# Attention in a fused three-layer kernel: the max pass two quarters ahead of the exp pass, shift rows placed quarter by quarter

## Time and profile before

| | us |
|---|---|
| median of three runs | 835.84 |
| the three runs | 838.26, 829.43, 835.84 |
| the profiled execution | 830.55 |
| its span, first to last instruction | 828.8 |

### The profile page before, as it was taken

One profiled execution on the slowest core, in us unless ns is written; L12 is line 12 of the kernel. 1 busy time (PEld: TensorE's weight loads), 2 busy tenths in 40 slices (PEclk: granted clock), 3 DMA queues, 4 the chain that ended last, 5 costly groups with the idle time before them and its releaser, 6 DMA issues.

```text
span 828.8 us, 23658 instructions
## 1 busy us (share of the span) xinstructions
PE 780.3 (94%) x6498; PEld 380.8 (46%) x6498; DVE 746.7 (90%) x2543; ACT 629.5 (76%) x1529; POOL 539.0 (65%) x838
## 2 busy tenths in 40 slices
PE   3999999989999999999999999999999998999997
PEld 2545544434444444454454454444444444445443
DVE  4899989989999999999999999999999848999996
ACT  2777777626888888888888888888878766677775
POOL 3787877865567566567567567467453336878887
PEclk9999999977999999999999999999999999999999
DMA  6700000332333233233233233233231000010011
GB/s 172 133 0 0 0 1 20 112 133 93 107 118 105 90 118 106 86 115 108 83 115 111 81 115 115 77 115 117 80 120 36 2 1 15 26 38 25 25 38 39
DMA packets 54969, 62.02 MB, mean 75 GB/s; under 512 B 5696, under 2 KB 48576, under 8 KB 54784
## 3 DMA queue, kind: packets, MB, share of 16 engines
q1 hardware_dynamic: 54912, 61.33, 23.2%
HBM read 31.70 MB, written 29.36 MB: 74 GB/s over the span
## 4 chain that ended last, share of the span: by engine, by line
PE 53%; DVE 16%; issue 7%; POOL 3%; ACT 2%; DVEq 1%; POOLq 0%; ACTq 0%
PE bank L1004 17%; PE bank L964 11%; DVE att_neg_max L1198 8%; PE bank L987 6%; PE bank L1019 4%; PE bank L1043 2%; PE bank L1023 2%; DVE x L561 2%; PE bank L303 2%; PE bank L310 2%; PE bank L967 2%; POOL moe_rstd L419 1%; DVE x L1241 1%; PE bank L1034 1%; PE bank L1017 1%
## 5 line engine op out<-in xcount | busy, mean ns | idle before, releaser
L1198 DVE TENSOR_REDUCE att_neg_max<-bank 128x1 bf16<-128x512 f32 (+3 forms) x704 | 407.9, 637 | 23.7 <-PE bank L967 20.2
L1077 ACT ACTIVATE att_probs<-bank 128x512 f32<-128x512 f32 x640 | 346.8, 596 | 64.1 <-PE bank L987 62.9
L1158 POOL TENSOR_SCALAR_AFFINE_SELECT att_probs<-att_probs 128x512 f32<-128x512 f32 x256 | 159.3, 634 | 201.1 <-ACT att_probs L1077 200.8
L987 PE MATMUL bank<-att_q_st,att_k_st 53*128 53x512 bf16 (+3 forms) x1024 | 210.6, 302 | 1.1 <-ACT att_probs L1077 1.1
L374 ACT ACTIVATE moe_scaled<-bank,moe_gates 128x128 f32<-128x128 f32 x512 | 145.2, 370 | 62.8 <-PE bank L310 57.0
L964 PE MATMUL bank<-att_k_st,att_q_st 51*128 51x384 bf16 (+2 forms) x768 | 180.3, 280 | 6.1 <-DVE att_neg_max L1198 4.6
L1004 PE MATMUL bank<-att_probs,att_v 128*32 128x512 f32 (+3 forms) x2048 | 177.3, 441 | 1.0 <-POOL att_probs L1158 0.4
L561 DVE SCALAR_TENSOR_TENSOR x<-bank,moe_gates,x 128x128 f32 (+1 forms) x512 | 160.4, 339 | 16.6 <-PE bank L303 15.7
L967 PE MATMUL bank<-att_k_st,att_q_st 64*128 64x128 bf16 x1024 | 159.3, 220 | 0.1
L964 PEld LDWEIGHTS bank<-att_k_st,att_q_st 51*128 51x128 bf16 x768 | 70.9, 95 | 177.5 <-DVE att_neg_max L1198 123.9
L303 PE MATMUL bank<-moe_we,moe_hT 128*128 128x512 f32 x256 | 134.2, 606 | 0.8 <-DVE x L1241 0.8
(11 more groups left out here) (83 smaller groups left out, 859.0 us busy)
## 6 DMA issues: line engine op xcount, KB each, us to landing
qk_parts<-att_parts SPq DMA_DIRECT2D x32, 384.0 KB, 2.5
att_q_st<-qk_parts SPq DMA_DIRECT2D x64, 192.0 KB
att_k_st<-qk_parts SPq DMA_DIRECT2D x64, 192.0 KB
qk_parts<-att_parts SPq DMA_DIRECT2D x32, 256.0 KB, 2.1
x<-in_L_attn_x SPq DMA_DIRECT2D x16, 256.0 KB, 2.8
qk_parts<-att_parts SPq DMA_DIRECT2D x32, 128.0 KB, 1.7
out<-x SPq DMA_DIRECT2D x16, 256.0 KB, 2.3
moe_we<-in_L_ffn_We SPq DMA_DIRECT2D x1, 512.0 KB, 4.9
```

The source lines that it names most:

```text
L987: mm = nc.tensor.matmul(exp_ps[m % RING][:, c:c + S - j * P], k_st[par][low:low + FINE_ROW, r, j * P:(j + 1) * P], q_st[par][low:low + FIN ...
L1077: nc.scalar.activation(probs[g % 2][:, n, :], exp_ps[m % RING][:], ACT.Exp).then_inc(exp_done, 1)
L1158: nc.gpsimd.affine_select(out=view, in_=view, compare_op=ALU.is_ge, fill=0.0, base=0, pattern=[[0, 4], [1, P]], channel_multiplier=-1).the ...
L1198: nc.vector.tensor_reduce(neg_max[par][:, g // 2, g % 2, heads[0]:heads[0] + len(heads), i], max_ps[m % RING][:, 0:len(heads) * width].rea ...
```

## The change

**Max pass.** It runs two quarters ahead: `on_max` does quarter g+2 of b while g is 0 or 1, and quarter g-2 of b+1 after that. **Sides.** `group_at` gives the half and the side of a quarter; the sides go 0, 1, 1, 0, so that max and exp quarters two apart still lie on different sides. **Shift rows.** One quarter (16 rows of the transpose, one row of `q_st`) at a time, four times a step, at slot 2 of each quarter: `shift1` at (0, 2), `shift2` at (1, 2), `shift3` at (2, 2) for quarters 1, 2 and 3 of b, `shift0` at (3, 2) for quarter 0 of b+1. The exp pass waits at the head of every quarter. **Second layer.** The pieces in `LATE` move, to follow the max pass, which now ends with quarter 1 of step 15.

```diff
 SIDE_WORK = [
-    {4: "project_q", 10: "project_k"},
-    {2: "shift_hi", 4: "turn_o1"},
-    {0: "turn_o", 4: "project_v"},
-    {0: "output", 2: "shift_lo", 4: "turn_o0", 10: "turn_h"},
+    {2: "shift1", 4: "project_q", 10: "project_k"},
+    {2: "shift2", 4: "turn_o1"},
+    {0: "turn_o", 2: "shift3", 4: "project_v"},
+    {0: "output", 2: "shift0", 4: "turn_o0", 10: "turn_h"},
 ]
...
-LATE = {(1, 0): "statistics0", (1, 4): "normalise0", (1, 8): "turn_h", (2, 0): "statistics1", (2, 3): "logits",
-        (2, 5): "normalise1", (2, 7): "exp_gap", (2, 9): "places", (3, 3): "gates"}
+LATE = {(0, 1): "statistics0", (0, 6): "normalise0", (2, 0): "turn_h", (2, 2): "statistics1", (2, 4): "logits",
+        (2, 6): "normalise1", (2, 9): "exp_gap", (3, 0): "places", (3, 3): "gates"}
...
+def group_at(g):
+
+    return g // 2, (g % 2) ^ (g // 2)
...
-                if on_max and g == 0 and there(b):
-                    on_max(b, par, half, GROUPS - 1, n)
-                if on_max and g > 0 and there(b + 1):
-                    on_max(b + 1, 1 - par, half + par, g - 1, n)
+                if on_max and g < 2 and there(b):
+                    on_max(b, par, half, g + 2, n)
+                if on_max and g >= 2 and there(b + 1):
+                    on_max(b + 1, 1 - par, half + par, g - 2, n)
...
-        def place_shift(b, par, half, hf):
+        def place_shift(b, par, half, g):
-            sp.wait_ge(side_read, use(b if hf else b - 1, "shift_hi" if hf else "shift_lo"))
-            pairs = slice(hf * PAIRS // 2, (hf + 1) * PAIRS // 2)
-            sp.dma_start(q_st[par][SHIFT_ROW:SHIFT_ROW + SIDE + 1:SIDE, pairs, :],
-                         shift[:]).then_inc(shift_in[par][hf], DMA)
+            sp.wait_ge(side_read, use(b if g else b - 1, f"shift{g}"))
+            half_at, ab = group_at(g)
+            pairs = slice(half_at * PAIRS // 2, (half_at + 1) * PAIRS // 2)
+            row = ab * SIDE + SHIFT_ROW
+            sp.dma_start(q_st[par][row:row + 1, pairs, :], shift[:]).then_inc(shift_in[par][g], DMA)
         def step(b, par, half):
             if there(b):
                 place_shift(b, par, half, 1)
+                place_shift(b, par, half, 2)
             if there(b + 2):
                 store_parts(b + 2, par, half + 1, 0)
+            if there(b):
+                place_shift(b, par, half, 3)
+            if there(b + 2):
                 store_parts(b + 2, par, half + 1, 1)
                 stack(b + 2, par, half + 1, 0)
...
-            if n == 0 and g in (0, 2):
-                pe.wait_ge(shift_in[par][g // 2], half * (SHIFT_DMAS * DMA) + SHIFT_DMAS * DMA)
+            if n == 0:
+                pe.wait_ge(shift_in[par][g], half * (SHIFT_DMAS * DMA) + SHIFT_DMAS * DMA)
```

More of the change, by code:

```diff
@@ L774, in attention @@
     neg_max = both(lambda i: sb(f"neg_max{i}", [P, 2, 2, PAIRS // 2, T], BF16))
-    shift = sb("shift", [T * H // 2, P], BF16)
+    shift = sb("shift", [T * PAIRS // 2, P], BF16)
     probs = both(lambda i: sb(f"probs{i}", [P, EXP_UNITS, S]))
@@ L799, in attention @@
     stack_in = both(lambda i: both(lambda hf: sem(f"stack_in{i}{hf}")))
-    shift_in = both(lambda i: both(lambda hf: sem(f"shift_in{i}{hf}")))
+    shift_in = both(lambda i: [sem(f"shift_in{i}{g}") for g in range(GROUPS)])
     SCRATCH_DMAS = 3
@@ L823, in present @@
             return True
-        offset = {"turn_h": 3, "project_q": 2, "project_k": 2, "project_v": 1, "shift_lo": 1, "shift_hi": 0,
+        offset = {"turn_h": 3, "project_q": 2, "project_k": 2, "project_v": 1, "shift0": 1, "shift1": 0, "shift2": 0, "shift3": 0,
                   "turn_o1": -1, "turn_o": -1, "output": -1, "turn_o0": 0}[what]
@@ L983, in take_exp_scores @@
                 pe.wait_ge(exp_done, (b - 1) * NE + (last + 1))
-            low = (g % 2) * SIDE
+            low = group_at(g)[1] * SIDE
             for hh, j, c in exp_unit(n):
@@ L992, in weigh_values @@
         def weigh_values(b, par, g, j):
-            half_at, ab = divmod(g, 2)
+            half_at, ab = group_at(g)
             if j == 0:
@@ L997, in weigh_values @@
                 pe.wait_ge(masked, b * NK + (g + 1) * MASK_UNITS)
-                if ab == 0 and (g > 0 or after(b, 0)):
+                if g % 2 == 0 and (g > 0 or after(b, 0)):
                     pe.wait_ge(pv_read, b * HALVES + half_at)
@@ L1004, in weigh_values @@
                 mm = nc.tensor.matmul(pv_ps[VW * hh:VW * (hh + 1), j * P:S], v[par][:, j, 4 * half_at + hh, ab, :],
-                                      probs[g % 2][:, n, c:c + S - j * P], start=(ab == 0 and j == 0),
-                                      stop=(ab == 1 and j == T - 1))
+                                      probs[g % 2][:, n, c:c + S - j * P], start=(g % 2 == 0 and j == 0),
+                                      stop=(g % 2 == 1 and j == T - 1))
             if j == T - 1:
@@ L1024, in side @@
                                           w["wv"][:], start=True, stop=True)
-            elif what in ("shift_lo", "shift_hi"):
-                hi = what == "shift_hi"
-                pe.wait_ge(max_read, (b if hi else b + 1) * NM + (NM if hi else NM // 2))
-                mm = nc.tensor.transpose(side_ps[0:T * H // 2, 0:P // 2].bitcast(BF16),
-                                         neg_max[par if hi else 1 - par][:, int(hi)], consts.ident_b)
+            elif what[:-1] == "shift":
+                g = int(what[-1])
+                half_at, ab = group_at(g)
+                pe.wait_ge(max_read, (b if g else b + 1) * NM + (g + 1) * MAX_UNITS)
+                mm = nc.tensor.transpose(side_ps[0:T * PAIRS // 2, 0:P // 2].bitcast(BF16),
+                                         neg_max[par if g else 1 - par][:, half_at, ab], consts.ident_b)
             elif what == "turn_o":
@@ L1103, in side @@
                                      scale=1.0 if s else HD ** -0.5).then_inc(side_read, 1)
-            elif what in ("shift_lo", "shift_hi"):
-                hi = what == "shift_hi"
-                if hi:
-                    act.wait_ge(shift_in[par][0], (half + 1) * (SHIFT_DMAS * DMA))
+            elif what[:-1] == "shift":
+                g = int(what[-1])
+                if g > 0:
+                    act.wait_ge(shift_in[par][g - 1], (half + 1) * (SHIFT_DMAS * DMA))
                 elif after(b, -1):
-                    act.wait_ge(shift_in[par][1], (half + 1) * (SHIFT_DMAS * DMA))
-                nc.scalar.activation(shift[:], side_ps[0:T * H // 2, 0:P // 2].bitcast(BF16),
+                    act.wait_ge(shift_in[par][GROUPS - 1], (half + 1) * (SHIFT_DMAS * DMA))
+                nc.scalar.activation(shift[:], side_ps[0:T * PAIRS // 2, 0:P // 2].bitcast(BF16),
                                      ACT.Copy).then_inc(side_read, 1)
```

4 lines of the change are left out of this document (2 added, 2 removed).

## The result

| | before | after |
|---|---|---|
| median of four runs | 835.77 us | 867.41 us |
| fastest to slowest | 829.43 to 838.26 | 859.87 to 874.5 |
| profiled execution (its span) | 830.55 (828.8) | 869.77 (868.0) |

What follows compares the result with a forecast made beforehand. PE and DVE were taken to hand each other the bound in the attention. 9.8 + 4.0 + 4.5 - 1.0 = 17.3 us on the profiled 830.55, plus 2.2 for an ordinary run, gave 850 us, range 833 to 864.

Steps and rivals of the forecast that it cites:

- Part 1: Head of quarter 1: PE waits for the shift row behind the stack, 14 x 0.7 = 9.8 us, bounds 0 to 19.6.
- So a row doesn't overtake a stack: SP's DMA queue: a shift row's packets move only with the last of the stack issued ahead of it.
- a sign against its reading of the queue: DMA packets: a shift row moving while the stack is in full flow would make the reading of the queue wrong.
- DVE's reserve: Head of quarter 1: DVE still has a unit to read while PE waits, for which 0.1 us was taken off.
- The price of 1.0 us: Quarter 1's wait, if stack takes 6 engines and row 16: nearer 1.0 us a step, sum 4 us higher.
- After that every step is as before: Steps after the start: unchanged, the saved quarter returning as max work in step 15, counted in the end's 4.5 us.
- the list of three things that change in a step: Every step: two more shift transposes, a new wait in front of quarter 1, a new one in front of quarter 3.
- Part 2: Two more transposes a step: free in quarter 0, 0.25 us in quarter 2, 16 x 0.25 = 4.0 us.
- Part 3: Step 15: second-layer work in DVE's full quarter 0 adds 3.3 us, `turn_h` waiting at quarter 2 1.2: 4.5 us.
- Part 4: Start: DVE waits for POOL's `att_rstd`, so little of the saved quarter is gained, -1.0 us (-2.4 to 0).
- the second rival: Start saved in full: exp pass about 7.2 us earlier, waits and ends free, 829.6 us; chance 0.10.
- Everything on the path: Whole attention: all 32 transposes count, 9.3 us, and waits are the longest, 19.6 us; about 865 us, chance 0.12.

Runs made afterwards that it cites:

- e1: Changed kernel with the stack of a second half issued a quarter later, behind the shift row of quarter 1: 850.71 us, 1.019 to before.
- e3: Changed kernel with both edits, stack behind the shift row of quarter 1 and ring of max banks begun anew at quarter 1: 839.63 us, 1.003 to before.
- e2: Changed kernel with the ring of max banks begun anew at the head of quarter 1 instead of quarter 2: 857.75 us, 1.027 to before.
- e5: Kernel before with only its ring of max banks begun anew at the head of quarter 2 instead of quarter 1: 839.51 us, 1.007 to before.
- e7: e6 with the second layer's pieces in step 15 moved later, meant to follow the max pass: 833.97 us, 0.9995.
- e6: e3 with, in step -1, POOL's root taken before its splits and the first shift row sent ahead of k's stores and the stack: 832.96 us, 0.9955.
- e8: e3 with the quarters visiting the sides 0, 1, 0, 1, so max and exp units of a slot share a side: 1380.2 us, 1.654.
- e9: Kernel before with the side order 0, 1, 1, 0 alone, lead of three quarters and shift rows as before: 885.59 us, 1.062.
- e4: Changed kernel with the shift row of quarter 1 issued by ScalarE on its own DMA queue, stack issued when it was: 852.59 us, 1.023.

## Why the prediction was wrong

**The base.** Of the 17.4 us between 850 and 867.41, 3.0 are the base: 830.55 + 2.2 = 832.75 us stood for an ordinary run of the kernel before, whose median is 835.77. The other 14.3 are the sum.

**Part 1, the wait at quarter 1: the mechanism right for the packets that PE waits for, the size too small.** 9.8 us predicted, 17.2 measured, and e1 returns 17.4. "So a row doesn't overtake a stack" holds for six of the row's 16 packets; the other ten move while the stack is in full flow, which the prediction named as a sign against its reading of the queue. The price doesn't change by it, since PE waits for the last packet. Three figures were low, which steps 2 to 14 show (step 1 grows by only 0.2 us). I took the tail of the stack as nothing in 6 of 14 steps and 0.2 to 1.1 us in the three that I named of the others, from the bytes that still moved *before* the change. After it the row's last packet comes 7.97 to 8.86 us into the step, 8.3 on average, and in no step of the 13 is it there when PE arrives, 7.9 us into the step or sooner. I took 0.66 us from there to the release of PE, which the earlier trace rows give as a lower end ("at least"; that row's last packet ended at 557.89 us, which makes it 0.87); after the change it is 0.57 to 1.07 us, 0.78 on average. Together that is a wait of 1.2 us and not 0.8, and the quarter grows by 1.3. And I took off 0.1 us for DVE's reserve, of which nothing shows. The price of 1.0 us, to which the Trainium skill's rule on six and 16 engines pointed, would have been the better choice.

**What failed: "After that every step is as before", and the list of three things that change in a step.** There is a fourth. A shorter lead moves not only which quarters run together, it also moves the seam between two sequences, and at the seam the ring of max banks is one unit short. That shows as 12.0 us in the quarters 1; taking it away brings 9.3 us (e3 against e1) or 11.8 (e2 against after), and alone, in the kernel before, it costs 7.3 (e5's loop, where quarter 2 has no added transpose). The rows of the order at the head of quarter 1 show max units that wait for `att_max_read`, without the number of the unit waited for. To see it I would have had to read the one line of code for the units below three, and to ask why PE did not wait there before; the rows put it down to `project_k`. With the ring's own price, the 7.3 us by which e5's loop is longer than that of before, and part 1 as measured, the sum is 17.2 + 7.3 + 4.0 + 4.5 - 1.0 = 32.0 us, beside 31.6 between the medians and 33.4 in the profiles. That it comes so near is in part luck. With the late row gone, the ring and the transposes together are 12.4 us of the loop (e1 against before), and how they share them depends on which is taken first: e3 takes 9.3 away with the ring and leaves 3.1, e5 gives the ring alone 7.3, which would leave 5.1.

**Part 2, the transposes: the size about right behind the ring's stall and too large without it, the sign by which to see it wrong.** I said 0.25 us in quarter 2, and that quarter 2 would grow by it. It grows by 0.02 (7.50 for 7.48 us). But e5 shows that a quarter 2 behind the ring's stall takes 7.20 us without the transpose, so that 0.30 us seem to be there and hidden. PE's timeline of the changed kernel in quarter 2, from the first exp unit to the product with v, 1.74 us:

```profile
566.32 0.38 PE L997 MATMUL bank<-att_q_st,att_k_st 53*128 53x512 bf16 x1
...
567.62 0.22 PE L977 MATMUL bank<-att_k_st,att_q_st 64*128 64x128 bf16 x1
567.98 0.22 PE L1040 MATMUL bank<-bf_consts,att_neg_max 128*16 128x128 bf16 x1
568.06 1.06 PE L1014 MATMUL bank<-att_probs,att_v 128*32 128x512 f32 x8
```

And of e5, 1.45 us, where no transpose stands between:

```profile
548.61 0.38 PE L990 MATMUL bank<-att_q_st,att_k_st 53*128 53x512 bf16 x1
...
549.91 0.22 PE L970 MATMUL bank<-att_k_st,att_q_st 64*128 64x128 bf16 x1
550.06 1.06 PE L1007 MATMUL bank<-att_probs,att_v 128*32 128x512 f32 x8
```

With the ring in its old place the price almost vanishes: quarter 2 grows by 0.08 us a step in e3, and outside step 0 its loop is 1.5 us longer than that of before, in 14 steps. That the difference between e5 and the changed kernel in quarter 2 is the transpose alone is argued from these rows; the two differ in lead and sides too.

**Part 3, the end: the total about right, in part by luck.** 4.5 us predicted, 4.8 measured to the first expert matmul. But of these 2.5 are in quarters 0 and 1, where 3.3 were forecast, and nothing in quarter 2, where the 1.2 us of `turn_h` should have shown; 2.2 us come behind quarter 2, where no term stood, some of it at the lower clock of the windows above. That DVE limits quarter 0 fits e7, where quarter 0 is 2.9 us shorter without the second layer's pieces (and at a granted clock of 1.00 for 0.82); what sets the end as a whole stays open.

**Part 4, the start: right,** -1.1 us for -1.0, for the reasons given, though the size was a choice within -2.4 to 0: DVE waits 4.84 us for `att_rstd`, and the first exp unit, which waits for the row behind the stack, starts 1.35 us after the first max unit. (The row's last packet ends at 191.62 us; the trace puts the wait down to DVE, for which that unit doesn't wait.) e6 takes both away and gains 5.3 of the 7.2 us that the second rival put on a full start.

**The rivals.** "Everything on the path" gave 865 us and so came nearest, half of it for the wrong reason: its wait of 1.4 us a step is near the 1.3 measured, but its 9.3 us of transposes took the place of the ring, and e3, which has all the transposes, is at most 3.1 us longer in the loop than before. The range's upper end was built from it, and no case in it had room for a term that I had not seen.

## What to carry to other kernels

When a schedule shifts one pass against another, look for the places where a count is not a multiple of its ring: the seam moves with the pass, and what hid it (here, by the rows, one projection of 1.13 us) stays where it was. Before a small transfer is put on the critical path, look at what stands ahead of it in its queue: reordering two DMAs was worth 17 us of the loop here, and giving the small one a queue of its own 12.6. And a quarter whose length is unchanged can hold two changes of opposite sign; a kernel with one of them alone tells them apart.

## What the runs showed of the hardware

- **The granted clock and the two halves of the array's rows.** In e8 all max and exp matmuls of a quarter lie on one half of the partitions; the granted clock is 0.50 from 171 us on, for over 1000 us, with PE busy in 17.87 of 17.87 us. In e9, with half of the quarters like that, it is 1.00 in the loop, but it rose only in the first quarter on two sides. The Trainium skill ("TensorE: Matmul & The Clock Gate", section "What's actually happening") says that the clock follows how busy TensorE has been; by that alone e8 would run at 2.4 GHz, and the measurement decides against it. Which property of e8's work the clock answers to was not tried further.
- **Sides.** Matmuls on different halves can start together (a max and an exp matmul at 186.53 us in e6), on the same half they follow one another (0.24 against 0.45 us a unit). With this agrees the Trainium skill ("TensorEngine Tiling (Array Packing)", section "Key Properties"), by which different tiles of the array can run at the same time.
- **A small transfer can end in two parts.** Behind the stack 10 of the row's 16 packets were done 4.4 us into the step and the last at 8.2; from another engine's queue (e4) the last six still came 2.4 to 3.2 us behind the first ten; with nothing in front (e1) all 16 moved within 0.3 us.
